# The rows of each token's lower expert fetched while the last expert is computed, and results kept on the chip

## The reference

```python
x = x + tanh(g_ffn[0]) * _L0_ffn_ref(layernorm(x), ...)   # 8 experts, square(relu), plus a shared expert
...
x = x + tanh(g_ffn[1]) * _L1_ffn_ref(layernorm(x), ...)   # 8 experts, silu(gate) * up, with biases
# both:
probs = softmax(logits)
topv, topi = top_k(probs, 2)         # two experts for each token
weights = topv / sum(topv)
y[token] = sum over the two: weights[k] * expert_{topi[k]}(x[token])
```

## Time and profile before

| | us |
|---|---|
| median of 3 runs | 1370.53 |
| lowest, highest run | 1364.76, 1375.53 |
| profiled execution: its time | 1368.85 |
| profiled execution: its span, first to last instruction | 1367.1 |
| PE busy in the span | 1127.2 (82%) |
| DVE, ACT, POOL busy | 750.6, 385.2, 359.7 |

### The profile page before, as it was taken

The page is one execution under the profiler, slowest core; times in us unless marked ns, Lnnn a source line. Parts: engine busy times, 40 slices in busy tenths (PEclk is TensorE's granted clock), DMA queues, the critical chain, the costliest instruction groups (busy, mean ns, idle before and its releaser), DMA issues.

```text
span 1367.1 us, 17137 instructions
## 1 busy us (share of the span) xinstructions
PE 1127.2 (82%) x5906; PEld 890.0 (65%) x5906; DVE 750.6 (55%) x1778; ACT 385.2 (28%) x705; POOL 359.7 (26%) x290
## 2 busy tenths in 40 slices
PE   2898989989866676899999968999999389999940
PEld 1646867567555664676877636868786179998930
DVE  5565754675734445555656554454546646666642
ACT  1204032041222323234242332332422033333310
POOL 4302244040411225321010132010101622224235
PEclk8899999999978988999999999999999789999975
DMA  7700014000256653100000010000000855535435
GB/s 263 261 1 31 0 53 148 0 1 1 80 167 202 168 157 119 35 28 0 1 0 0 16 51 27 0 1 0 0 1 3 264 167 184 181 103 183 147 104 173
DMA packets 91890, 113.66 MB, mean 83 GB/s; under 512 B 6576, under 2 KB 77488, under 8 KB 91696
## 3 DMA queue, kind: packets, MB, share of 16 engines
q1 hardware_dynamic: 72480, 78.46, 17.6%
q0 software_dynamic: 19344, 34.35, 8.7%
HBM read 76.09 MB, written 36.70 MB: 83 GB/s over the span
## 4 chain that ended last, share of the span: by engine, by line
PE 54%; DVE 18%; POOL 8%; issue 7%; DMA 5%; ACT 5%; SPq 3%; DVEq 0%; POOLq 0%; ACTq 0%
PE PS L198 12%; PE PS L200 11%; PE PS L199 11%; PE PS L1659 6%; PE PS L1549 4%; POOL routed L777 4%; PE PS L1520 4%; DMA xg<-routed 3%; POOL HB L837 2%; DVE S L1072 2%; POOL rstd L770 2%; DVE st L1053 1%; DVE SM L1343 1%; PE PS L1425 1%; PE PS L1577 1%
## 5 line engine op out<-in xcount | busy, mean ns | idle before, releaser
L770 POOL TENSOR_TENSOR rstd<-ve,minus_half 128x4 f32<-128x4 f32 x40 | 40.6, 1014 | 398.9 <-DVE ve L1060 248.8
L198 PE MATMUL PS<-xt,split 128*128 128x256 f32 x412 | 122.4, 297 | 13.3 <-issue 10.2
L1431 PE MATMUL PS<-ones_bf 128*128 128x512 bf16 x424 | 111.5, 410 | 16.3 <-DMA routed<-S,dest 16.3
L199 PE MATMUL PS<-xt,split 128*128 128x256 f32 x412 | 120.3, 292 | 0.0
L200 PE MATMUL PS<-xt,split 128*128 128x256 f32 x412 | 120.0, 291 | 0.0
L456 POOL TENSOR_TENSOR split<-raw,split 128x1024 fp32r<-128x1024 f32 (+1 forms) x15 | 66.6, 4442 | 139.4 <-DMA raw<-down_w 84.2
L198 PEld LDWEIGHTS PS<-xt,split 128*128 128x128 f32 x412 | 83.2, 202 | 16.7 <-issue 12.9
L1659 PE MATMUL PS<-VP,HB 128*128 128x257 f32 x384 | 85.8, 382 | 4.4 <-DVE VP L1356 4.4
L198 PE MATMUL PS<-split,hs 128*128 128x256 f32 x244 | 79.4, 325 | 11.1 <-DVE hs L516 9.6
L1431 PEld LDWEIGHTS PS<-ones_bf 128*128 128x128 bf16 x424 | 42.3, 105 | 70.9 <-issue 38.4
L777 POOL DMA_INDIRECT routed<-S,dest x64 | 66.4, 1038 | 68.1 <-DVE dest L1139 50.3
(11 more groups left out here) (301 smaller groups left out, 2748.9 us busy)
## 6 DMA issues: line engine op xcount, KB each, us to landing
xg<-routed SPq DMA_DIRECT2D x44, 256.0 KB, 2.8
outputs<-y SPq DMA_DIRECT2D x40, 256.0 KB, 3.6
outputs<-zeros SPq DMA_DIRECT2D x3, 2048.0 KB, 16.1
routed<-zeros SPq DMA_DIRECT2D x20, 256.0 KB, 3.0
raw<-m_w SPq DMA_DIRECT2D x16, 256.0 KB, 5.9
split<-m_w POOLq DMA_DIRECT2D x16, 256.0 KB, 5.0
x_base<-X SPq DMA_DIRECT2D x8, 512.0 KB, 3.8
raw<-gate_w SPq DMA_DIRECT2D x8, 512.0 KB, 8.2
```

The lines of the kernel that those rows point to most:

```text
L198: pe.matmul(out_, a[1], b[0], start=first, stop=False)
L199: pe.matmul(out_, a[0], b[1], start=False, stop=False)
L770: pool.tensor_tensor(rstd[h][:], ve[h][:], minus_half[:], ALU.pow).then_inc(sem("rstd_ready"), 1)
L1431: pe.matmul(free.rearrange("p (a b) -> p a b", b=P), ones_bf[:], ones_bf[:].unsqueeze(1).to_broadcast([P, TT, P]), start=True, stop=True)
```

## The change

Each token's two expert numbers are put in order: `choose` takes their minimum and maximum, and finds the probability that belongs to each by a masked sum. The gathers of the lower-numbered experts' rows (they can't belong to expert 7) wait only until the groups of experts 0 to 6 are stored (`all_but_last`), and are issued on POOL ahead of `all_stored`; the gathers of the higher ones come after it. In MoE 0 that is so for pair 0; pair 1 is fetched as before. In MoE 1 it holds for all four sequences: the fetched rows have room of their own (`rows_of`, all of HB[0] and HB[1]), the residuals stay in X and EMB (`result`) in place of the store to `x_base[1]` and the load from it, and DVE adds first all lower rows, then the upper ones as each sequence's rows land. `raw_k` moves from HB to S0, so that POOL no longer waits for `gt_ps`.

```diff
+        def rows_of(n, kk):
+            return HB[kk][:, 2 * n:2 * n + 2].rearrange("p a (j d) -> p (a j) d", d=D)
+        def result(n, h):
+            return X[h] if n < 2 else EMB[h]
...
+            sp.wait_ge(sem("batch_c"), B)
+            raw_in(sp, 1, 0)
-            for pair in range(PAIRS):
-                if pair == PAIRS - 1:
-                    sp.wait_ge(sem("batch_c"), B)
-                    raw_in(sp, 1, 0)
-                for n, h in of_pair[pair]:
-                    sp.wait_ge(sem("batch_c"), n + 1)
-                    sp.dma_start(x_base[1, n].rearrange("(j p) d -> p j d", p=P), X[h][:]).then_inc(sem(f"x_out{h}"), 16)
-            for h in two:
-                sp.wait_ge(sem(f"x_out{h}"), 16 * 2 * PAIRS)
...
-                    sp.dma_start(X[h][:], x_base[1, n].rearrange("(j p) d -> p j d", p=P)).then_inc(sem(f"x_in{h}"), 16)
...
-            def gather(m, n, h):
+            def gather(n, kk, rows, name):
                 for j in range(TT):
-                    for kk in range(2):
-                        pool.indirect_dma_start(out=rows_h[h][:, kk, j], out_offset=None, in_=outputs,
+                    pool.indirect_dma_start(out=rows[:, j], out_offset=None, in_=outputs,
...
+            def all_but_last(m):
+                pool.wait_ge(sem("source"), m + 1)
+                stored = pool.value_load(table[m][0:1, 2 * E - 2:2 * E - 1], min_val=1, max_val=NG)
+                pool.wait_ge(sem(f"m{m}_yout"), 16 * stored + 1)
+                pool.sem_inc(sem("passed"), 1)
...
+            all_but_last(0)
+            for h in two:
+                gather(h, 0, rows_h[h][:, 0], f"rows{h}")
             pool.wait_ge(sem("cw_hi"), 16)
             pool.wait_ge(sem("cw_raw"), 80)
             all_stored(0)
             for stage, n, h, it, q in stages_c("pool"):
                 if stage == "gather":
-                    if n == 1:
-                        after(pool, "gt_ps")
                     if n >= 2:
                         pool.wait_ge(sem("combined"), n - 1)
-                    gather(0, n, h)
+                        gather(n, 0, rows_h[h][:, 0], f"rows{h}")
+                    gather(n, 1, rows_h[h][:, 1], f"rows{h}")
...
             moe_pool(pool, 1)
+            all_but_last(1)
+            for n in range(B):
+                gather(n, 0, rows_of(n, 0), "rows0")
             all_stored(1)
-            for pair in range(PAIRS):
-                for n, h in of_pair[pair]:
-                    if pair:
-                        pool.wait_ge(sem("combined"), B + n - 1)
-                    gather(1, n, h)
+            for n in range(B):
+                gather(n, 1, rows_of(n, 1), f"upper_rows{n}")
...
-                step(dve.tensor_copy(R[:, 3, :, 0:2], rix[h][:, :, 0:2]))
-                step(dve.tensor_copy(expert_of[:, n], rix[h][:, :, 0:2]))
+                step(dve.tensor_copy(R[:, 3, :, 2:4], rix[h][:, :, 0:2]))
+                chained()
+                step(dve.tensor_tensor(R[:, 3, :, 0:1], R[:, 3, :, 2:3], R[:, 3, :, 3:4], ALU.min))
+                step(dve.tensor_tensor(R[:, 3, :, 1:2], R[:, 3, :, 2:3], R[:, 3, :, 3:4], ALU.max))
...
+                step(dve.tensor_copy(expert_of[:, n], R[:, 3, :, 0:2]))
                 step(dve.reciprocal(R[:, 7, :, 5], R[:, 7, :, 4]))
-                chained()
+                for kk in range(2):
+                    step(dve.tensor_tensor(R[:, 6 * kk], R[:, 4 + kk], R[:, 1], ALU.mult))
+                chained()
+                for kk in range(2):
+                    step(dve.tensor_reduce(R[:, 2, :, kk], R[:, 6 * kk], AX, ALU.add))
...
+            dve.wait_ge(sem("rows0"), 16 * TT * (2 * PAIRS + B))
+            for _, n, h in pairs:
+                step(add_rows(n, h, 0))
+            chained()
+            for _, n, h in pairs:
+                dve.wait_ge(sem(f"upper_rows{n}"), 16 * TT)
+                add_rows(n, h, 1).then_inc(sem("combined"), 1)
```

More of the change, by code:

```diff
@@ L107, in sem @@
             return sems[name]
-        x_base = nc.dram_tensor("x_base", (2, B, T, D), F32, kind="Internal").ap()
+        x_base = nc.dram_tensor("x_base", (B, T, D), F32, kind="Internal").ap()
         routed = [nc.dram_tensor(f"routed{m}", (XROWS, D), F32, kind="Internal").ap() for m in range(2)]
@@ L707, in _ @@
                     sp.wait_ge(sem("batch_a"), n + 1)
-                    sp.dma_start(x_base[0, n].rearrange("(j p) d -> p j d", p=P), X[h][:]).then_inc(sem(f"x_out{h}"), 16)
+                    sp.dma_start(x_base[n].rearrange("(j p) d -> p j d", p=P), X[h][:]).then_inc(sem(f"x_out{h}"), 16)
                     if n + 2 < B:
@@ L731, in _ @@
             moe_sp(sp, 1, lambda sp: raw_in(sp, 1, 1))
[L732 to L739 removed]
+            for _, n, h in pairs:
+                sp.wait_ge(sem("combined"), B + n + 1)
+                sp.dma_start(out[n].rearrange("(j p) d -> p j d", p=P), result(n, h)[:]).then_inc(sem(f"x_out{h}"), 16)
             for h in two:
[L741 removed]
+                sp.wait_ge(sem(f"x_out{h}"), 16 * 2 * PAIRS)
         @block.gpsimd
@@ L1272, in _, with combine @@
             moe_dve(dve, 0)
-            def combine(m, n, h):
-                x_t = residual(n, h) if m == 0 else X[h]
-                if m == 0 and n >= 2:
+            def combine(n, h):
+                x_t = residual(n, h)
+                if n >= 2:
                     dve.wait_ge(sem(f"second_in{h}"), 32)
                 else:
-                    dve.wait_ge(sem(f"x_in{h}"), 16 * (PAIRS + 1) + (m and 16 * (n // 2 + 1)))
-                dve.wait_ge(sem(f"rows{h}"), 16 * 2 * TT * (m * PAIRS + n // 2 + 1))
+                    dve.wait_ge(sem(f"x_in{h}"), 16 * (PAIRS + 1))
+                dve.wait_ge(sem(f"rows{h}"), 16 * 2 * TT * (n // 2 + 1))
                 for kk in range(2):
                     for j in range(TT):
-                        ins = dve.scalar_tensor_tensor(out=x_t[:, j], in0=rows_h[h][:, kk, j], scalar=share[m][:, n, j, kk:kk + 1],
+                        ins = dve.scalar_tensor_tensor(out=x_t[:, j], in0=rows_h[h][:, kk, j], scalar=share[0][:, n, j, kk:kk + 1],
                                                        in1=x_t[:, j], op0=ALU.mult, op1=ALU.add)
@@ L1290, in combine, with add_rows @@
                             chained()
+            def add_rows(n, h, kk):
+                for j in range(TT):
+                    ins = dve.scalar_tensor_tensor(out=result(n, h)[:, j], in0=rows_of(n, kk)[:, j], scalar=share[1][:, n, j, kk:kk + 1],
+                                                   in1=result(n, h)[:, j], op0=ALU.mult, op1=ALU.add)
+                return ins
             after(dve, "gt_hi")
@@ L1307, in _ @@
                 if stage == "combine":
-                    combine(0, n, h)
+                    combine(n, h)
                 elif stage == "slots":
@@ L1394, in _ @@
                     dve.wait_ge(sem("final_ps"), n + 1)
-                    if n >= 2:
-                        dve.wait_ge(sem(f"x_out{h}"), 16 * (PAIRS + 1))
-                    step(dve.scalar_tensor_tensor(out=X[h][:].rearrange("p j d -> p (j d)"), in0=banks(h, 0).rearrange("p b t -> p (b t)"),
+                    step(dve.scalar_tensor_tensor(out=result(n, h)[:].rearrange("p j d -> p (j d)"), in0=banks(h, 0).rearrange("p b t -> p (b t)"),
                                                   scalar=tanh_g[:, 1:2], in1=residual(n, h)[:].rearrange("p j d -> p (j d)"), op0=ALU.mult, op1=ALU.add))
                     chained()
-                    spread(h, X[h], 1e-5)
+                    spread(h, result(n, h), 1e-5)
                 elif stage == "final":
-                    scaled_to(h, X[h], S2[h], lambda ins: ins.then_inc(sem("batch_c"), 1))
+                    scaled_to(h, result(n, h), S2[h], lambda ins: ins.then_inc(sem("batch_c"), 1))
                 elif stage == "xnT":
@@ L1413, in _ @@
             moe_dve(dve, 1)
-            for pair in range(PAIRS):
-                for n, h in of_pair[pair]:
-                    combine(1, n, h)
+            dve.wait_ge(sem("rows0"), 16 * TT * (2 * PAIRS + B))
+            for _, n, h in pairs:
+                step(add_rows(n, h, 0))
+            chained()
+            for _, n, h in pairs:
+                dve.wait_ge(sem(f"upper_rows{n}"), 16 * TT)
+                add_rows(n, h, 1).then_inc(sem("combined"), 1)
         @block.tensor
```

11 lines of the change are left out of this document (4 added, 7 removed).

## The result

The changed kernel takes 1354.23 us (median of four executions, 1350.42 to 1357.24), the kernel before 1370.26 in the same comparison (1364.76 to 1375.53). The ratio is 0.9882, interval 0.9836 to 0.9928: 16 us (10 to 22), a gain of 1.2%. The profiled execution of the changed kernel is the fastest of its four (1350.42, span 1348.3).

A forecast was written before the change was run, and what follows sets the result against it. POOL's issue of 32 gathers in a row was taken to bound the tail. The terms -20.7 + 3.45 + 0.4 + 0.4 = -16.4 gave 1352.4 from the profiled execution, 1354.1 from the median; forecast 1353, range 1345 to 1363.

The forecast's parts named there:

- the rest of the change: Costs outside the tail: choice of experts 3.45, last expert of MoE 0 0.4, start of part C 0.4.
- additions that hold POOL for over 3 us in all: Sign of being wrong: tail additions on DVE delay POOL's gathers by over 3 us; 1.15 was forecast.
- a choice that costs above 5: Sign of being wrong: sorting the expert numbers costs above 5 us; 3.45 was forecast.
- The tail (-20.7): End of MoE 1: 16 lower gathers go before the last store lands, so the span ends 20.7 us earlier.
- The choice (+3.45): Added DVE steps in `choose` cost 0.69 us in each of five places on the path, 3.45 in all.
- The last expert of MoE 0 (+0.4): Eight early gathers beside fetches and stores delay the last store by 0.4 us, between 0 and 6.
- the start of part C (+0.4): `WHH` on POOL moves earlier and holds `gbias` instead of `KK`; `KK` of sequence 1 ends 0.4 us later.
- the hold of `gbias`: Start of part C: `WHH` on POOL holds `gbias`, and `RT` behind it, making them 2.0 us late.
- The overlap doesn't happen: Rival: lower gathers start only after MoE 1's last store, all 32 in a row; 1373, chance 0.05.
- The choice hides: Rival: PE's and ACT's answers cover most added DVE work, 1.0 in place of 3.45; 1350, chance 0.13.
- The last experts are slowed: Rival: fetches and stores beside gathers take twice as long, 6 to 8 us lost; 1360, chance 0.14.
- slower, by the clock: Rival: a fetch over 9.3 us in expert 7 idles PE and its clock falls; 1378, chance 0.03.

The follow-up runs named there:

- the first batch: Choice alone, spread additions, one-operand additions and late share, run on one chip beside before at 1382.62; ratios 1.0043, 1.0014, 1.0024, 1.0005.
- three kernels that contain it: Changed kernel with spread additions, with lower additions replaced by one-operand products, or with share moved behind `dest`: 1384.16, 1386.13, 1383.94; ratios 1.0014, 1.0024, 1.0005.
- the second run: The changed kernel repeated unchanged beside the kernel before on the same chip: 1351.26, ratio 0.9875.
- the third run: The changed kernel unchanged, in a third comparison on another chip: 1353.40, ratio 0.9902 to before.
- the late share: Changed kernel with reciprocal, products, sums and `share` moved behind `dest`: 1383.94, ratio 1.0005; again on the third chip 1349.74, 0.9874.
- the first comparison: The changed kernel against the kernel before, on a chip not on record: 1354.23 against 1370.26, ratio 0.9882.
- the other two batches: Second: after repeated and each overlap removed, before at 1370.02. Third: after, choice alone, late share, late share with spread additions, before at 1366.76.
- the third chip: Chip of the third batch, before at 1366.76: after 0.9902, choice alone 1.0043, late share 0.9874, late share with spread additions 0.9862.
- the spread additions: Changed kernel with only two sequences' lower additions first in the tail, each of the others behind an upper one: 1384.16, ratio 1.0014.

## Why the prediction was right

1353 was forecast and 1354.2 measured; the sum gave -16.4 and the medians -16.0. The mechanism is the one forecast: the kernel without the early gathers in MoE 1 loses the whole gain. That the sum fits to 0.4 us is luck in part, since the measured gain is itself known only as 10 to 22. The overlap was put at 20.7, and taking it out cost 24 by the medians and 21 by the means (16 to 26); the rest of the change was put at 4.25, and measured 4.5 and 5.9, each with some 3 or 4 either way. In the profiled pair the tail gave 17.8, less than forecast, and chance between the two runs covers the costs. It is luck too that the comparison was not made on a chip like that of the first batch, if the kernel after behaves there as three kernels that contain it did. And two of the prediction's own signs of being wrong came true: additions that hold POOL for over 3 us in all (3.9 in the profiled execution), and a choice that costs above 5 (5.9 twice, though both intervals begin near 2.5). By its steps:

- **The tail (-20.7).** Right in kind and nearly in size. The lower gathers began at 1296.2, the uppers 3.73 after the issue of the last store, where 3.9 was forecast, but for another reason: the prediction took 2.2 for the landing and 1.0 for the read of `table` and seven waits behind the sixteenth gather (no run shows its 0.15 for one small instruction). The landing took 2.94 beside the gathers, and the reads and waits cost nothing that shows. In the two further runs of after the tail is 32.1 and 32.9 us, 19.8 to 20.6 less than 52.7. In the profiled one it is 17.8 less. There the additions held POOL longer: 1.15 was forecast for all gathers, and one of them alone was held 3.1 (4.05 for 0.95). That term depends on the run: 1.2 in all in the second run, and one gather of 3.26 again in the kernel without the overlap in MoE 1. The last gather's landing was put at 3.02 and took 3.48 here and 4.06 in the third run.
- **What the held gather says of the rule.** The Trainium skill's page "SBUF — State Buffer" (Who interferes with whom) infers that an operation with two operands in SBUF doesn't hold up the making of descriptors. The rows of after speak against it (1.21 and 4.05 in place of 0.95 beside such additions), as did those of before; the last section has a clearer case.
- **The choice (+3.45).** The steps came as forecast: 0.65 for one place against 0.69. The whole effect was measured at 5.9 twice, with 3.45 inside both intervals but near their lower end; the term is probably too small.
- **The last expert of MoE 0 (+0.4) and the start of part C (+0.4).** Both were small, and the sign of the second was wrong. From the last store of `y` to the first `combine` 29.50 us went by before and 28.98 after. The first term came about as forecast: the store landed after 2.7 in place of 2.1, and the product of `WIH` (L1298, L1315) began 13.7 us after the store's issue in place of 13.2, 0.5 later. Counted from that store, `WHH` began at 13.2 where 13.7 was forecast (519.1 less 505.41), and met `gbias` as forecast. But it held it for 0.7 only, where the prediction put 2.0, since `gbias` came only 0.9 before `WHH` was done. So `RT` started 1.3 later than before (0.5 and 0.7), not 2.4; `KK` of sequence 1 lost its hold of 1.6 and ended at 29.1 in place of 29.6. The mis-sized term is the hold of `gbias`: 2.0 forecast, 0.7 measured, and with it 0.4 of loss became 1.0 of gain. Without the early gathers in MoE 0 the time is the same within some 5 us, so the runs can't tell either term from nothing.
- **Rivals.** "The overlap doesn't happen" was built as the kernel without it in MoE 1: 1375.2, about as priced (1373). "The choice hides" (1.0 us) fell: the choice alone cost 5.9, at least 2.5. "The last experts are slowed" and "slower, by the clock" did not occur in MoE 1 in any run of after (127 matmuls in 19.9 us, clock 0.96 to 1.00). A stronger form of both did on the first batch's chip, with a cause that the prediction didn't have: PE waited for nothing that the profile shows, not for fetched rows, and the stretch's clock fell to 0.83 with it. There kernels that contain the change were no faster than before.

## What to carry to other kernels

When a row of gathers ends a kernel and its issue is the limit, ask which of them depend on data that is complete earlier, and order the choice so that half of them can go before the last store; the work that the order costs should then stand behind the results that others wait for. In a change of several parts take each out alone: here one overlap is the whole gain, a second one and the dropped traffic are worth nothing that could be measured, and the sorted choice is the price. And repeat on another chip before a gain of 1% is trusted: one and the same kernel, that with the late share, gave 0.9874 and 1.0005.

## What the runs showed of the hardware

**PE idle beside a row of indirect DMAs, on one chip only.** While POOL issued sixteen gathers at 1.25 us each, PE on that chip ran a few matmuls and then waited 0.8 to 1.7 us, with no semaphore behind it. In the profiles of three kernels this lost 14 to 15 us in expert 7 (9.0 of it are waits in the one read above, beside a mean clock of 0.83), and 5 to 6 in the last expert of MoE 0. In all six profiles of the first comparison and the other two batches that have these gathers, they cost the same matmuls nothing (127 in 19.9 us, clock 0.96 to 1.00; the stores of `y` come 9.6 and 10.6 us apart, as before).

The early gathers aren't needed for it. The kernel with the choice alone has none, and at the end of part A it has sixteen scatters in a row, which are indirect DMAs too. The last of them and the first fetch of MoE 0, on the chip of the first batch:

```profile
378.94 0.96 POOL L777 DMA_INDIRECT routed<-S,dest  x1 [0.30 <-issue]
388.82 0.41 SPq L399 DMA_DIRECT2D xg<-routed  x1
```

and the same kernel on the third chip:

```profile
376.77 0.96 POOL L777 DMA_INDIRECT routed<-S,dest  x1 [0.30 <-issue]
380.02 0.41 SPq L399 DMA_DIRECT2D xg<-routed  x1
```

9.9 us against 3.3. On that chip the other three kernels need 7.1 to 9.9 for the same step, and every profile of the other comparisons shows 3.2 to 4.2. Its waits of PE without a releaser are more as well (us in total, times, longest):

```profile
PE PS L198 <- issue: 17.3, 18, 2.3
```

and the only such line of the same kernel on the third chip:

```profile
PE PS L198 <- issue: 10.4, 14, 2.3
```

The longest such wait of that profile, 11.9 us until 1107.38, is no loss: on the third chip the same matmuls wait 14.95 us, there for the scatters. Before was slower on the first batch's chip too, 1382.6 against 1370.0 and 1366.8. A loss beside scatters would fit, but that isn't shown. That PE's instructions arrive late because the traffic of the indirect DMAs shares their way is only argued. The DMA rows of the kernel with the spread additions list a single transfer of the kind "instruction" between 1302 and 1356, ahead of the gathers, and none among PE's gaps; so the trace neither shows it nor tells it from other causes.

**An indirect DMA that POOL begins while DVE runs a long operation is held until DVE is done.** The clearest case, here in the profile of before, at the end of part C:

```profile
1081.18 3.64 POOL L777 DMA_INDIRECT routed<-S,dest  x1 [0.30 <-issue]
1080.64 3.35 DVE L456 TENSOR_TENSOR split<-raw,split 128x3072 fp32r<-128x3072 f32 x1
```

Twelve of the fourteen profiles have it, with 3.47 to 4.10 us for a scatter that takes 0.96 alone; in the other two no scatter begins while this operation runs. One that is under way already when DVE begins is hardly held (0.96 in five profiles, 1.12 and 1.13 in two). The held one is done 0.8 us after DVE: 1084.82 here after 1083.99, 523.05 after 522.24 (`RT`), 1325.20 after 1324.39 in the tail of after. An unheld one takes 0.95, so nearly all of its work seems to come after DVE's end. Both operands and the result of these operations are in SBUF; which of them does it was not taken apart.

**How long short additions hold a gather is chance.** Beside the same 16 additions the longest gather took 4.05 us in one run of the kernel after and 1.28 in two others. The long hold covers all eight additions that were left, as if they were one operation; what decides between the two isn't shown.
